# Four tiles in place of two for the shifted quads of a gated stage, the first four fetched by the attention's program

## The reference, cut to what matters

```python
def shift_token(t):
    t1, t2 = jnp.split(t, 2, axis=-1)
    t2 = jnp.pad(t2, ((0, 0), (1, 0), (0, 0)))[:, :-1]
    return jnp.concatenate([t1, t2], axis=-1)

def _layer(x, wqkv, qs, ksc, wo, lg, lb, w1, b1, w2, b2):
...
    x = x + o @ wo
    h = shift_token(x)
    mu = h.mean(-1, keepdims=True)
    var = h.var(-1, keepdims=True)
    h = (h - mu) / jnp.sqrt(var + 1e-05) * lg + lb
    h = h @ w1 + b1
    a, g = jnp.split(h, 2, axis=-1)
    h = a * jax.nn.gelu(g, approximate=False)
    x = x + h @ w2 + b2
    return x
```

## Time and profile before

| what | value |
|---|---|
| median of 3 runs | 4139.81 us (4138.38 to 4140.43) |
| profiled execution | 4138.42 us, span 4136.7 us |
| TensorE matmul busy | 3886.4 us, 94% |
| VectorE, ScalarE, GpSimd busy | 73%, 69%, 44% |
| the two attentions, about | 1142 to 1697, 1856 to 2401 us |
| the two gated stages, about | 1698 to 1856, 2401 to 2559 us |

### The profile page before, as it was taken

How to read it: one execution, slowest core, us unless ns; L and a number is a source line. 1 busy time by engine, 2 the same in 40 slices (tenths; PEclk the granted TensorE clock), 3 DMA queues, 4 the chain that set the end, 5 groups by cost and what they waited for, 6 DMA issues and landing times. The chain is left out here.

```text
span 4136.7 us, 106732 instructions
## 1 busy us (share of the span) xinstructions
PE 3886.4 (94%) x33992; PEld 3010.0 (73%) x33992; DVE 3010.7 (73%) x7586; ACT 2847.9 (69%) x6420; POOL 1807.6 (44%) x1724
## 2 busy tenths in 40 slices
PE   8999899999979999798999979999999989998999
PEld 5676678888756666685666668888888867776777
DVE  6888655555479999558999945777777767776665
ACT  5666455555579999657999965777777767775333
POOL 3333222222268888426777743333333321112443
PEclk9999999999999999999999999999999989999999
DMA  0000100000100000100000011000000000000000
GB/s 18 9 9 9 48 7 6 6 6 6 41 9 8 8 8 8 24 19 10 8 8 8 12 25 31 1 0 0 0 0 0 0 3 4 3 3 6 12 12 13
DMA packets 109251, 42.38 MB, mean 10 GB/s; under 512 B 91232, under 2 KB 107872, under 8 KB 108512
## 3 DMA queue, kind: packets, MB, share of 16 engines
q1 hardware_dynamic: 109152, 41.10, 3.9%
HBM read 20.16 MB, written 4.19 MB: 6 GB/s over the span
## 5 line engine op out<-in xcount | busy, mean ns | idle before, releaser
L1129 POOL TENSOR_TENSOR l_rc<-l_rc,l_rs 128x1024 f32<-128x1024 f32 x128 | 303.7, 2373 | 201.1 <-DVE l_rs L1321 199.4
L1196 ACT ACTIVATE l_prob<-l_prob,l_mx 128x128 f32<-128x128 f32 x1024 | 312.0, 390 | 0.0
L1802 POOL TENSOR_TENSOR mb_steps<-w_upto,mb_dta 128x1024 f32<-128x1024 f32 x64 | 121.5, 1898 | 359.4 <-DVE mb_dta L2054 359.4
L699 POOL TENSOR_TENSOR ca_prob<-ca_prob,ca_sm 128x1232 f32<-128x1232 f32 x64 | 144.0, 2250 | 299.4 <-DVE ca_sm L865 299.4
L1221 PE MATMUL l_qk_ps<-w_local,l_hT 128*128 128x512 f32 x512 | 248.8, 609 | 12.9 <-DVE l_rs L1321 11.5
L1123 POOL TENSOR_TENSOR l_prob<-l_prob,l_sm 128x1024 f32<-128x1024 f32 x128 | 243.0, 1898 | 18.2 <-DVE l_sm L1307 18.2
L1106 POOL TENSOR_TENSOR l_rc<-l_rc,l_ss 128x1024 f32<-128x1024 f32 x128 | 243.7, 1904 | 12.5 <-POOL l_rc L1129 4.5
L1955 PE MATMUL mb_x_ps<-w_wx,mb_xT 128*128 128x256 f32 x1024 | 237.8, 385 | 0.0
L1316 DVE TENSOR_REDUCE l_ss<-l_sq 128x16 f32<-128x1024 f32 x128 | 156.1, 1219 | 76.6 <-ACT l_sq L1160 76.4
L2513 POOL TENSOR_TENSOR mo_hid<-mo_hid,mo_gate 128x1024 f32<-128x1024 f32 x64 | 121.8, 1903 | 199.7 <-DVE mo_hid L2659 199.7
L1955 PEld LDWEIGHTS mb_x_ps<-w_wx,mb_xT 128*128 128x128 f32 x1024 | 190.7, 191 | 23.4
(11 more groups left out here) (351 smaller groups left out, 12045.2 us busy)
## 6 DMA issues: line engine op xcount, KB each, us to landing
la_xin<-in_x SPq DMA_DIRECT2D x64, 64.0 KB, 1.8
l_h<-lt_y SPq DMA_DIRECT2D x128, 32.0 KB
lt_quad<-lt_y SPq DMA_DIRECT2D x32, 128.0 KB
out_x<-k_x SPq DMA_DIRECT2D x64, 64.0 KB, 1.5
l_h<-lt_y SPq DMA_DIRECT2D x128, 31.8 KB
lt_quad<-lt_y SPq DMA_DIRECT2D x32, 127.0 KB
ca_ctxT<-in_ctx_T SPq DMA_DIRECT2D x128, 19.2 KB
wr_state<-in_p_state SPq DMA_DIRECT2D x1, 2438.5 KB, 12.1
```

Source lines behind the costliest of these rows:

```text
L1129: gp.tensor_tensor(wide(rc[l][:]), wide(rc[l][:]), wide(rs[l][:]), ALU.add).then_inc(*pool_sum.did("rot"))
L1196: ex = sc.activation(p[:, a, j], p[:, a, j], ACT.Exp, bias=mx[l][:, a, j:j + 1])
```

## The change

There are four quad tiles and four semaphores for each layer. The attention fetches quads 0 to 3 for the gated stage that follows; the gated stage fetches quad q after the centring of quad q - 4, into tile q modulo 4. The gated pipelines have turn 4 (8 steps unrolled, two trips over 4, five steps unrolled). The attention clears a row of each of the four tiles, ahead of its other memsets but two. In the gated stage ScalarE's start waits for one memset (`eps`) and VectorE's for none; both wait for all five ahead of gate work in the unrolled steps.

```diff
@@ Batch
+    def paired(self, k):
+        fixed = self.base // 4 * k + k
+        return fixed if self.trip is None else self.trip * (self.turn // 4 * k) + fixed
@@ local_attention
-        NZERO = 8
+        NZERO = 10
...
-                for quad in (0, 1):
+                for quad in range(4):
                     sp.wait_ge(*vec_y.at("y", Batch(4 * quad + 3)))
                     shifted_quad(sp, g, layer, quad, quad)
...
+                for slot in range(4):
+                    gp.memset(g.quads[slot][0:1], 0.0).then_inc(zeroed, 1)
                 for l in (0, 1):
                     gp.memset(h[l][:], 0.0).then_inc(zeroed, 1)
-                    gp.memset(g.quads[l][0:1], 0.0).then_inc(zeroed, 1)
@@ gated_mlp
-        pool_norm = Stage(m.sem("pool_norm"), "c n")
+        pool_norm = Stage(m.sem("pool_norm"), "c n", reach=4)
...
-                    if b and not (b.trip is None and b.base < 2):
+                    if b and not (b.trip is None and b.base < 4):
                         index = b.index if b.trip is None else sp.snap(b.index)
-                        sp.wait_ge(*pool_norm.at("c", b, ago=2))
-                        shifted_quad(sp, g, layer, index, b.lane)
-
-                pipeline(sp, g.NB // Q, OUT + 1, step)
+                        sp.wait_ge(*pool_norm.at("c", b, ago=4))
+                        shifted_quad(sp, g, layer, index, b.slot)
+
+                pipeline(sp, g.NB // Q, OUT + 1, step, turn=4)
...
-                        gp.tensor_tensor(off[l][:], h[l][:], mv[l][:, :, 0].unsqueeze(2).to_broadcast([T, Q, C]),
+                        gp.tensor_tensor(off[l][:], h[b.slot][:], mv[l][:, :, 0].unsqueeze(2).to_broadcast([T, Q, C]),
...
@@ gated_mlp, scalar
-                sc.wait_ge(zeroed, NZERO)
+                sc.wait_ge(zeroed, 1)
                 sc.wait_ge(g.fetched, g.NLOCAL)
 
                 def gate(b, half):
                     sc.wait_ge(*pe_gate[half].at("ag", b))
                     sc.wait_ge(*vec_gate[half].at(f"u{half}{CH - 1}", b, ago=1))
+                    if b.trip is None:
+                        sc.wait_ge(zeroed, NZERO)
...
@@ gated_mlp, vector
-                v.wait_ge(zeroed, NZERO)
                 v.wait_ge(g.fetched, g.NLOCAL)
 
                 def gate(b, half):
                     v.wait_ge(*pe_out[half].at("o", b, ago=1))
+                    if b.trip is None:
+                        v.wait_ge(zeroed, NZERO)
...
-                        v.wait_ge(h_in[l], b.loaded(32))
+                        v.wait_ge(h_in[b.slot], b.paired(32))
                         for i in range(Q):
-                            v.bn_stats(stats[l][:, i], h[l][:, i]).then_inc(*vec_stat.did(f"s{i}"))
+                            v.bn_stats(stats[l][:, i], h[b.slot][:, i]).then_inc(*vec_stat.did(f"s{i}"))
...
@@ local_transformer
-        g.quads = both(m, "quad", [T, 4, C])
-        g.quad_in = [m.lanes(f"quad_in{layer}_") for layer in (0, 1)]
+        g.quads = [m.sb(f"quad{slot}", [T, 4, C]) for slot in range(4)]
+        g.quad_in = [[m.sem(f"quad_in{layer}_{slot}") for slot in range(4)] for layer in (0, 1)]
```

More of the change, by code:

```diff
@@ L1454, in step @@
                             gate(b, half)
-                pipeline(sc, g.NB // Q, OUT + 1, step)
+                pipeline(sc, g.NB // Q, OUT + 1, step, turn=4)
             @block.tensor
@@ L1503, in step @@
                         out(b, 0)
-                pipeline(te, g.NB // Q, OUT + 1, step)
+                pipeline(te, g.NB // Q, OUT + 1, step, turn=4)
             @block.vector
@@ L1556, in step, with shifted_quad @@
                         add(b, 0)
-                pipeline(v, g.NB // Q, OUT + 1, step)
-def shifted_quad(sp, g, layer, index, lane):
+                pipeline(v, g.NB // Q, OUT + 1, step, turn=4)
+def shifted_quad(sp, g, layer, index, slot):
     low = g.y[:, bass.ds(index * 4, 4), 0:C // 2]
     high = g.y[0:T - 1, bass.ds(index * 4, 4), C // 2:C]
-    sp.dma_start(g.quads[lane][:, :, 0:C // 2], low).then_inc(g.quad_in[layer][lane], 16)
-    sp.dma_start(g.quads[lane][1:T, :, C // 2:C], high).then_inc(g.quad_in[layer][lane], 16)
+    sp.dma_start(g.quads[slot][:, :, 0:C // 2], low).then_inc(g.quad_in[layer][slot], 16)
+    sp.dma_start(g.quads[slot][1:T, :, C // 2:C], high).then_inc(g.quad_in[layer][slot], 16)
 def local_transformer(nc, g):
```

5 lines of the change are left out of this document (4 added, 1 removed).

## The result

The changed kernel takes 4111.54 us, the median of four runs (4109.69 to 4113.86); the kernel before took 4139.84 beside it (four runs, 4138.38 to 4140.43). The ratio is 0.9932, with a 95% interval of 0.9915 to 0.995: faster by 0.7%, 28.3 us by the medians. The forecast was 4114.2 in a range of 4110 to 4121. The profiled execution of the changed kernel took 4113.86 us (span 4112.2), the slowest of its four.

A forecast was written before the change was run, and what follows sets the result against it. TensorE was taken to set the pace in a gated stage's long run, VectorE's load waits to delay its start. Gated starts -27.4 and memsets +1.8 gave -25.6 us, hence 4114.2 us, range 4110 to 4121.

The forecast's parts named there:

- Fetched ahead: Gated stages' start: quads 0 to 3 land 7.6 us before the attention's last addition, so 32.7 us of VectorE waits go.
- What is late next: Gated start rerun without load waits: ScalarE's and TensorE's chains give the second quad's gate product 13.7 us earlier per layer.
- t0: The time of the gated program's first memset, from which the prediction counts each gated stage's start.
- the sign of being wrong: Gated start: the prediction is wrong if ScalarE's chain has a wait that the DMA waits hide today.
- an unknown end: First 24 gate matmuls: a clock rising sooner, worth up to 1.7 us a layer, allowed for below the forecast.
- Clock at this point: Between first output product and second quad's gate product: clock stays up, so the piece takes 1.35 us, not 2.69.
- The rival with the fallen clock: Gated starts: TensorE's clock falls in both layers, gain 24.6 instead of 27.4, 4117.0 us; chance 0.16.
- the one with TensorE at half speed in steps 3 to 6: Each gated stage: TensorE stays at 1.2 GHz, a step takes 16.6 us; 4164.0 us at three steps per layer; chance 0.03.
- Four loads in flight, and turn of four: Gated stages' later steps: no later load is waited for, and fewer loop trips give some tenths at most; both taken as zero.
- The rival of reloaded code: Gated loops: each trip back reloads code as the body is twice as long, +4.6 us, 4118.8; chance 0.05.
- Memsets: Each attention's start: two more memsets shift everything behind them by 0.92 us per layer, +1.8 in all.
- The sign "either attention longer by more than 1 us": Attentions of both layers: the prediction is wrong if either takes longer by more than 1 us.

The follow-up runs named there:

- e2: The changed kernel, but the attention fetches only quads 0 and 1, the gated program quads 2 and 3; 4137.71 us, ratio 1.0002 to the kernel before.
- e1: The changed kernel, but ScalarE and VectorE again wait for all five memsets at the gated program's start; 4111.69 us, ratio 0.9938 to the kernel before.
- e8: The changed kernel with 18 unused identity transposes first on TensorE and six fewer ScalarE table loads per gated start; 4113.33 us, ratio 0.9941 to before.
- e9: The changed kernel run and profiled once more, with nothing altered; 4111.91 us, ratio 0.9936 to the kernel before.
- e3: The changed kernel, but ScalarE loads each table once for a gated stage's first four quads, six loads fewer; 4111.03 us, ratio 0.9936 to before.
- e6: The changed kernel, but the quad rows are cleared once, in the first attention, off the attentions' start; 4112.79 us, ratio 0.9938 to the kernel before.
- e10: The changed kernel with the upper half of every shifted load, quads and h, issued as 112 and 15 partitions; 4112.94 us, ratio 0.9936 to before.

## Why the prediction was right, point by point

**Fetched ahead: right, in place and size.** The first four loads lie as reckoned, at the rate of 7.65 us, and land some 8 us early where 7.6 was worked out. All 32.7 us of waits are gone, and no new one came. e2 shows the cause.

**What is late next: both engines later than worked out, off by 1.0 and 0.6 us.** The step gave TensorE's gate products the time from t0 + 6.6 to t0 + 13.8 (its terms add up to 13.7), a bit ahead of ScalarE (first gelu t0 + 12.8, output product t0 + 14.8). Both chains missed their terms:
- ScalarE's first gelu: 13.27 in both layers, right behind its last table load, as said, but 0.47 late. ScalarE started at 0.28 and not at 0.1, and its first logarithm waited 0.46 us for VectorE's statistics; each further quad took 3.13 to 3.14 us, close to the 3.17 taken. That wait is the sign of being wrong that the prediction had named (a wait in ScalarE's chain that the DMA waits hid), in a small size. By this chain the output product could start at 15.28.
- Start of TensorE's gate products: 7.26 and 7.11 in place of 6.6. VectorE's statistics start 0.69 us after GpSimd's first memset, in place of 1.13 before: 0.44 earlier and not 1.0; the row in the changed kernel says that GpSimd's L95 ended the idle time before them. That line gives a semaphore its first counts, here those of GpSimd's `n` that VectorE waits for ahead of its statistics, and it stands in GpSimd's program behind the five memsets. So taking away VectorE's wait for the memsets left a second wait on the same engine. The prediction looked at the first alone, and e1 puts the worth of its removal at 0.2 to 0.6 us, not 1.0.
- Their length: 7.09 was taken over from the row before, 8.23 and 7.98 measured. The clock had risen 3.4 us into them before and rises more than 4.8 us into them now. The prediction had named an earlier rise as an unknown end and had not named a later one. In the nine profiles with four quads fetched ahead the length lies between 7.57 and 8.48 us, but for the 5.45 of e8.

So TensorE ended at 15.49 and 15.09 instead of 13.8 and was the later of the two, by 0.5 us in layer 0 and by 0.1 in layer 1 (in the second profile, e9, ScalarE was). The output product followed at 15.76 and 15.36 instead of 14.8, and the second quad's gate product at 17.11 and 16.70 instead of 16.1. Each gated stage is shorter by 12.72 and 13.13 us, not 13.7: 1.5 us too much in the sum.

**Clock at this point: right.** It stays at 1.00 from 1714 on and the piece to the next gate product takes 1.35 us (1716.69 to 1718.04), the value taken, and not 2.69. The rival with the fallen clock is out, and the one with TensorE at half speed in steps 3 to 6 as well: the first step is 8.30 us at 1.00.

**Four loads in flight, and turn of four: right at zero.** No statistics wait for a later quad; a step takes 8.30 us; TensorE idles 2.15 us in the stretch with all trips, as before (2.11). The rival of reloaded code is not seen, though 61 packets in place of 57 show that more code is fetched. The rule of the Trainium skill's page "Runtime: NRT & Kernel Launch", section "Instruction fetch mechanics", weighed in the prediction, changed no time that these traces show.

**Memsets: right in place and in price, hidden in the sum.** The first h load goes out 0.90 us later in layer 1, ScalarE's first logarithm 0.91 later in layer 0, as said (0.92). Yet the attentions changed by +0.53 and -0.21, +0.3 in sum in place of +1.8; in e9's profile by +1.03 and -0.46, +0.6. In attention 0 the seven profiles with four rows cleared and `h` loaded as before lie between 555.38 and 555.97, mean 555.80, the two with two rows at 554.85 and 554.95: 0.9 more, and the changed kernel's own profile happens to be the lowest of the seven. (The sign "either attention longer by more than 1 us" is met in five of the seven, by this price alone.) In attention 1 two memsets cost 0.9 to 1.3 us between profiles of the same clock, but the profile of before had the lower clock from 27 to 36 us after the start and that of the changed kernel the higher, and this weighs 1.1 to 1.5 us the other way. The prediction had no term for the clock in the attentions; e2, which has the four memsets and the lower clock, shows that the memsets do not decide it.

**Rest: not zero.** 1575.88 in place of 1577.03. Nothing was changed there, and the ten experiments lie between 1575.52 and 1576.62, 0.4 to 1.5 us below. The kernel before has one profile, so this may be its chance; e2, as long as before up to here, is the nearest to it. In the state-space stage's first 40 us the granted clock is 0.92 against 0.87 in the profile before. No run singles it out.

**The sum.** Predicted were -27.4 + 1.8 = -25.6 us. The profiled spans differ by 24.5: -25.85 in the gated stages, +0.32 in the attentions, -1.15 behind and +2.18 of chance ahead. The medians differ by more, 28.3, because the profiled run of before was 1.4 below its median and that of the changed kernel 2.3 above. With e9 and the near variants e1 and e3 on two other sets of runs the change is worth 26.4 to 28.3 us, 0.8 to 2.7 more than forecast; of this the rest's 1.2 us are seen in profiles, and what is left is within the spread of single runs. The range held, and it held for its reasons in the main term. That the profiled spans come within 1.1 us of the forecast is luck in part: 1.5 us of gain too much in the gated stages stand against 1.5 us in the attentions, most of which is the clock of one stretch that happened to differ between two profiles; 2.2 us of chance ahead and 1.15 us behind were in no term.

## What to carry to other kernels

Before giving a late load more tiles and an earlier issue, ask why it takes so long: a transfer over 127 partitions, cut into 112 and 15, was there after 3.7 us in place of 10.02, and that edit alone, with no new tile, brought 24.2 us where the early fetch brought 26.4 to 27.1 on the same chip. When a wait is taken away, run the start again for each engine with the clock that it will have there, not with the one that its row had behind the wait. And price an edit of a microsecond from the lengths of single programs, between profiles whose granted clock is the same in each stretch: by medians e6, e8 and e10, which moved 0.8 to 3.1 us at a stage's start, show nothing, and by lengths in one pair of profiles the four more memsets of both attentions seemed to cost 0.3 us, where between profiles of the same clock it is 1.8 or more.

## What the runs showed of the hardware

- A DMA whose outermost size is 127 partitions ran on what looks like one DMA engine: 7.65 us for each quad, share 0.08, 18 GB/s; as 112 + 15 it was there 3.7 us after its issue, share 0.29, 64 GB/s.
- 24 equal matmuls in a row took between 5.45 and 8.48 us according to when the granted clock rose; in one kernel the same preparation gave 5.45 in one layer and 8.44 in the other.
- Attention 1 was 1.1 to 1.5 us longer in the six profiles with 0.81 granted from 27 to 36 us after its start than in those with 1.00 and as many memsets; kernels with the same start fell into either group.
- A part that no edit touched (0 to 1143 us) ended 2.2 us later in one profile, with 0.82 in place of 0.90 granted from 510 to 545 us, and between 1140.42 and 1145.55 in twelve.
